# Narrowing the subtracted softmax maximum to one bf16 number, and turning a unit's maxima by one transpose

## What is computed

```python
def _attend(q, k, v):
    sim = jnp.einsum('bhid,bhjd->bhij', q, k) * HD ** (-0.5)
    attn = jax.nn.softmax(sim, axis=-1)
    out = jnp.einsum('bhij,bhjd->bhid', attn, v)
```

## Time and profile before

| what | value |
|---|---|
| runs, median (lowest to highest) | 4588.85 us (4585.59 to 4595.32) |
| span of the profiled execution | 4575.9 us |
| median of the runs less that span | 12.95 us |
| PE busy | 4083.6 us (89%) |
| DVE busy | 3089.2 us (68%) |
| ACT busy | 2075.6 us (45%) |
| POOL busy | 1348.3 us (29%) |
| chain that ended last, by engine | PE 62%, DVE 16%, ACT 6%, issue 5% |

### The profile page before, as it was taken

One profiled execution on the slowest core, in us unless ns is written; L12 is line 12 of the kernel. 1 busy time (PEld: TensorE's weight loads), 2 busy tenths in 40 slices (PEclk: granted clock), 3 DMA queues, 4 the chain that ended last, 5 costly groups with the idle time before them and its releaser, 6 DMA issues.

```text
span 4575.9 us, 56543 instructions
## 1 busy us (share of the span) xinstructions
PE 4083.6 (89%) x20828; PEld 2493.2 (54%) x20828; DVE 3089.2 (68%) x4613; ACT 2075.6 (45%) x3756; POOL 1348.3 (29%) x664
## 2 busy tenths in 40 slices
PE   7999989789998887998999977888999999997889
PEld 5343346633334575555555546667555555546668
DVE  5888856688886666778777854345677777774355
ACT  2555544355565443444444435553344344444541
POOL 1100001100000124655655553421344444451120
PEclk8999989999998998999999988999999999998999
DMA  4223231123222333233223313223322232214220
GB/s 129 40 43 49 44 58 35 43 30 56 40 30 53 63 58 65 64 65 66 60 63 65 65 47 77 70 58 73 69 65 65 61 70 66 58 34 121 67 53 19
DMA packets 154420, 269.87 MB, mean 59 GB/s; under 512 B 36459, under 2 KB 70053, under 8 KB 153121
## 3 DMA queue, kind: packets, MB, share of 16 engines
q1 hardware_dynamic: 154144, 266.25, 27.7%
HBM read 105.01 MB, written 29.64 MB: 29 GB/s over the span
## 4 chain that ended last, share of the span: by engine, by line
PE 62%; DVE 16%; ACT 6%; issue 5%; POOL 4%; SPq 4%; DMA 3%; DVEq 0%; POOLq 0%; ACTq 0%
PE PS L1012 26%; PE PS L1191 12%; PE PS L1088 4%; PE PS L1084 4%; PE PS L1233 3%; PE PS L1321 3%; DVE t L1751 3%; PE PS L1243 2%; SPq L2181 2%; DVE t L1747 2%; POOL t L2042 1%; SPq L2198 1%; ACT t L1487 1%; DMA t<-t 1%; PE PS L1218 1%
## 5 line engine op out<-in xcount | busy, mean ns | idle before, releaser
L1012 PE MATMUL PS<-t 128*128 128x512 f32 (+4 forms) x7896 | 1981.4, 383 | 166.5 <-ACT t L1466 24.9
L1466 ACT ACTIVATE t<-PS 128x512 f32<-128x512 f32 (+2 forms) x1600 | 1166.6, 750 | 1175.6 <-PE PS L1012 1169.8
L1012 PEld LDWEIGHTS PS<-t 128*128 128x128 f32 (+2 forms) x7896 | 1246.0, 187 | 719.5 <-issue 260.2
L1191 PE MATMUL PS<-t 128*32 128x512 f32 (+2 forms) x4352 | 809.1, 610 | 0.2
L1747 DVE TENSOR_REDUCE t<-PS 128x1 fp32r<-128x1024 f32 x512 | 621.7, 1219 | 267.6 <-PE PS L1084 260.9
L1751 DVE TENSOR_REDUCE t<-PS 128x1 f32<-128x512 f32 x1024 | 650.8, 682 | 72.1 <-PE PS L1088 70.8
L2042 POOL TENSOR_TENSOR t<-t 128x1024 f32<-128x1024 f32 x256 | 617.6, 2412 | 130.4 <-ACT t L1466 103.4
L1088 PE MATMUL PS<-t 96*128 96x512 bf16 x1024 | 371.6, 395 | 33.9 <-DVE t L1751 14.8
L1084 PE MATMUL PS<-t 128*128 128x512 f32 x1024 | 338.6, 413 | 56.1 <-DVE t L1747 36.9
L2038 POOL TENSOR_TENSOR t<-t 128x1024 f32<-128x1024 f32 x64 | 155.1, 2424 | 747.5 <-PE PS L1201 448.7
L1191 PEld LDWEIGHTS PS<-t 128*32 128x32 f32 (+2 forms) x4352 | 170.6, 121 | 329.2 <-issue 324.5
(11 more groups left out here) (133 smaller groups left out, 3932.6 us busy)
## 6 DMA issues: line engine op xcount, KB each, us to landing
t<-t SPq DMA_DIRECT2D x640, 128.0 KB, 2.5
t<-scr_n SPq DMA_DIRECT2D x288, 128.0 KB, 6.5
t<-t SPq DMA_DIRECT2D x128, 256.0 KB, 3.9
scr_n<-t SPq DMA_DIRECT2D x72, 256.0 KB, 2.3
t<-t SPq DMA_DIRECT2D x256, 64.0 KB, 2.1
t<-in_L_Wg SPq DMA_DIRECT2D x16, 768.0 KB, 4.6
t<-in_L_W SPq DMA_DIRECT2D x36, 256.0 KB, 3.3
t<-in_L_Wo SPq DMA_DIRECT2D x64, 128.0 KB, 2.6
```

Of the source, the lines that this page charges most:

```text
L1012: ins = e.matmul(out, l, r, start=i == 0, stop=i == len(terms) - 1, tile_position=tp)
L1191: ins = e.matmul(banks[S.ot][wd * j:wd * j + wd, :], u.v[j][kt], P[0:S.pr, j, :], start=kt == 0, stop=kt == S.nkt - 1, tile_position=(0, w ...
L1466: e.activation(dst, src, ACT.Exp, scale=S.L.scale).then_inc(*expd.inc((S.i, i)))
```

## The change

The self and cross stages of layers 0 and 1 keep one bf16 number for the maximum instead of three. The self stages write it directly from the joining `tensor_reduce` (step `mjoin`); the cross stages write it directly from the block reductions, so no step is left between the last of them and the transpose. `MT` has two buffers there instead of one. Contractions go from 99 rows to 97. In all three kinds of stage the maxima of a unit lie side by side as columns of `MT` (16, 32 or 8 of them), one transpose turns them all, and one copy of 128 columns brings them to `MR`. Each partition of `MR` then holds 128 query rows of one head. The DMA of a head gathers four such partitions into one row. In the narrow cross stage one DMA gathers all 32 into the four rows, which lie behind each other on one partition. In the wide stages the maximum stays float32.

```diff
-            S.NM, S.NR = sbt(c, [128, 32]), sbt(c, [128, 32])
-            S.MT = sbt(c, [128, 8, 4, 3], BF16)
-            S.MR = [sbt(c, [12, N], BF16) for _ in range(2)]
+            S.MT = [sbt(c, [128, 32], BF16) for _ in range(2)]
+            S.MR = [sbt(c, [32, 128], BF16) for _ in range(2)]
+            sbt(c, [128, 976])
...
-            S.MT = [sbt(c, [128, S.nqt, 2], F32R) for _ in range(2)]
-            S.MR = [sbt(c, [2, 128 * S.nqt], F32R) for _ in range(2)]
+            S.MT = [sbt(c, [128, 2 * S.nqt], F32R) for _ in range(2)]
+            S.MR = [sbt(c, [2 * S.nqt, 128], F32R) for _ in range(2)]
+            sbt(c, [128, 768])
...
-                u.mrow = [buf[96:99, 0, j, q0:q0 + nw] for j in range(4)] if u.su is u else None
+                u.mrow = [buf[96:97, 0, j, q0:q0 + nw] for j in range(4)] if u.su is u else None
+                if cross and u.mrow:
+                    u.mrow = [buf[96:97, 0, :, :].rearrange("p j n -> p (j n)")]
...
-        return out + [("mparts", S, m), ("mturn", S, m)]
+        return out + [("mturn", S, m)] if S.cross else out + [("mjoin", S, m), ("mturn", S, m)]
...
# TensorE, mturn
+                elif S.cross:
+                    for j, q0 in ((2, 4), (3, 0), (3, 4)):
+                        k, nth = where["max", S.i, m, j, q0]
+                        w.wait_ge(bank_free[k], nth)
                 else:
-                    w.wait_ge(max_part, (S.i, m, "end"))
+                    w.wait_ge(max_part, (S.i, m))
                 w.wait_ge(set_up, "ident")
-                rows, idt = (12, identb) if S.L.style == 16 else (2, ident)
-                for q0 in range(0, S.nqt, 4):
-                    o, k, nth = take(w, small, ("turn", S.i, m, q0))
-                    o = o.bitcast(BF16) if S.L.style == 16 else o
-                    for q in range(4):
-                        if S.L.style == 16:
-                            src = S.MT[:, q0 + q, :, :].rearrange("p j c -> p (j c)")
-                        else:
-                            src = f(S.MT[m % 2][:, q0 + q, :])
-                        ins = e.transpose(o[0:rows, 128 * q:128 * q + 128], src, idt[:, :])
-                    ins.then_inc(*bank_full[k].inc(nth))
+                n = S.nqt * S.nh
+                o, k, nth = take(w, small, ("turn", S.i, m))
+                if S.L.style == 16:
+                    ins = e.transpose(o.bitcast(BF16)[0:n, 0:128], S.MT[m % 2][:, 0:n], identb[:, :])
+                else:
+                    ins = e.transpose(o[0:n, 0:128], f(S.MT[m % 2][:, :]), ident[:, :])
+                ins.then_inc(*bank_full[k].inc(nth))
...
# VectorE, narrow
-                    e.memset(S.QK[0][96:99, 1, :, :], 1.0).then_inc(*zeroed.inc((S.i, 0)))
+                    e.memset(S.QK[0][96:97, 1, :, :], 1.0).then_inc(*zeroed.inc((S.i, 0)))
...
-                e.tensor_reduce(S.NM[:, 8 * j + q0:8 * j + q0 + 4], v, AX.X, ALU.max, negate=True
-                                ).then_inc(*bank_free[k].nth(nth))
-            elif what == "mparts":
+                ins = e.tensor_reduce(S.MT[m % 2][:, 8 * j + q0:8 * j + q0 + 4], v, AX.X, ALU.max, negate=True)
+                ins.then_inc(*bank_free[k].nth(nth))
+            elif what == "mjoin":
...
-                e.tensor_copy(part[0], nm).then_inc(*max_part.inc((S.i, m, 1)))
-                w.wait_ge(max_part, (S.i, m, 1))
-                e.tensor_tensor(nr, nm, part[0], ALU.subtract).then_inc(*max_part.inc((S.i, m, 2)))
-                w.wait_ge(max_part, (S.i, m, 2))
-                e.tensor_copy(part[1], nr).then_inc(*max_part.inc((S.i, m, 3)))
-                w.wait_ge(max_part, (S.i, m, 3))
-                e.tensor_tensor(part[2], nr, part[1], ALU.subtract).then_inc(*max_part.inc((S.i, m, "end")))
+                e.tensor_reduce(S.MT[m % 2][:, 0:n], S.NMX[:, 0:n, :], AX.X, ALU.max, negate=True
+                                ).then_inc(*max_part.inc((S.i, m)))
...
# VectorE, mturn
-                for q0 in range(0, S.nqt, 4):
-                    o, k, nth = full(w, ("turn", S.i, m, q0))
-                    o = o.bitcast(BF16) if S.L.style == 16 else o
-                    e.tensor_copy(mr[:, 128 * q0:128 * q0 + 512], o[0:rows, 0:512]).then_inc(*bank_free[k].nth(nth))
+                o, k, nth = full(w, ("turn", S.i, m))
+                o = o.bitcast(BF16) if S.L.style == 16 else o
+                e.tensor_copy(mr[0:n, :], o[0:n, 0:128]).then_inc(*bank_free[k].nth(nth))
...
# SyncE, mturn
-                per = 3 if S.L.style == 16 else 1
-                mr = S.MR[m % len(S.MR)]
-                for j in range(S.nh):
-                    src, dst = mr[per * j:per * j + per, 0:128 * S.nqt], u.mrow[j]
+                mr = S.MR[m % 2]
+                per = S.nqt if S.L.style == 64 or not S.cross else 4 * S.nqt
+                for i, row in enumerate(u.mrow):
+                    src, dst = mr[per * i:per * i + per, :], row
                     if S.L.style == 64:
                         src, dst = f(src), f(dst)
-                    e.dma_start(dst, src).then_inc(*mrow_in[m % 2].inc((S.i, m), 16))
+                    e.dma_start(dst.rearrange("p (q n) -> p q n", n=128), src).then_inc(*mrow_in[m % 2].inc((S.i, m), 16))
```

More of the change, by code:

```diff
@@ L331, in attention_tiles @@
             T = S.after
-            S.P, S.OR, S.R, S.RE, S.NMX, S.NM, S.NR, S.MT, S.MR, S.NR2 = (
-                T.P, T.OR, T.R, T.RE, T.NMX, T.NM, T.NR, T.MT, T.MR, T.NR2)
+            S.P, S.OR, S.R, S.RE, S.NMX, S.MT, S.MR, S.NR2 = (
+                T.P, T.OR, T.R, T.RE, T.NMX, T.MT, T.MR, T.NR2)
             S.NAT, S.nqk, S.nbuf = T.NAT, 1, 4
@@ L1573, in scalar_program, with turn_read @@
                     w.wait_ge(r, a[0])
+    def turn_read(w, S, m):
+        old, last = (S, m - 2) if m >= 2 else (S.after, len(S.after.sus) + m - 2) if S.after else (None, 0)
+        if old:
+            k, nth = where["turn", old.i, last]
+            w.wait_ge(bank_full[k], nth)
     def vector_program(e, w):
@@ L1743, in vector_program @@
                     if m >= 2:
-                        k, nth = where["turn", S.i, m - 2, 0]
+                        k, nth = where["turn", S.i, m - 2]
                         w.wait_ge(bank_full[k], nth)
                     o, k, nth = full(w, ("max", S.i, m, j, qt))
-                    e.tensor_reduce(S.MT[m % 2][:, qt, j:j + 1], o, AX.X, ALU.max, negate=True
+                    e.tensor_reduce(S.MT[m % 2][:, S.nqt * j + qt:S.nqt * j + qt + 1], o, AX.X, ALU.max, negate=True
                                     ).then_inc(*bank_free[k].nth(nth))
@@ L1759, in vector_program @@
+                ins.then_inc(*bank_free[k].nth(nth))
+            elif what == "mjoin":
                 S, m = a
-                for key in [x for x in where if x[0] == "max" and x[1:3] == (S.i, m)][-3:]:
-                    k, nth = where[key]
+                turn_read(w, S, m)
+                n = S.nqt * S.nh
+                for j, qt, half in ((3, 2, 1), (3, 3, 0), (3, 3, 1)):
+                    k, nth = where["max", S.i, m, j, qt, half]
                     w.wait_ge(bank_free[k], nth)
-                nq = S.nqt
@@ L1764, in vector_program @@
-                n = nq * S.nh
-                if not S.cross:
-                    e.tensor_reduce(S.NM[:, 0:n], S.NMX[:, 0:n, :], AX.X, ALU.max, negate=True
-                                    ).then_inc(*max_part.inc((S.i, m, 0)))
-                    w.wait_ge(max_part, (S.i, m, 0))
-                nm = S.NM[:, 0:n].rearrange("p (j q) -> p j q", q=nq)
-                if m or S.after:
-                    old = S if m else S.after
-                    for q0 in range(0, old.nqt, 4):
-                        k, nth = where["turn", old.i, m - 1 if m else len(old.sus) - 1, q0]
-                        w.wait_ge(bank_full[k], nth)
@@ L1775, in vector_program @@
-                part = [S.MT[:, 0:nq, :, i].rearrange("p q j -> p j q") for i in range(3)]
-                nr = S.NR[:, 0:n].rearrange("p (j q) -> p j q", q=nq)
-                e.tensor_copy(part[0], nm).then_inc(*max_part.inc((S.i, m, 1)))
-                w.wait_ge(max_part, (S.i, m, 1))
-                e.tensor_tensor(nr, nm, part[0], ALU.subtract).then_inc(*max_part.inc((S.i, m, 2)))
-                w.wait_ge(max_part, (S.i, m, 2))
-                e.tensor_copy(part[1], nr).then_inc(*max_part.inc((S.i, m, 3)))
@@ L1782, in vector_program @@
-                w.wait_ge(max_part, (S.i, m, 3))
-                e.tensor_tensor(part[2], nr, part[1], ALU.subtract).then_inc(*max_part.inc((S.i, m, "end")))
+                e.tensor_reduce(S.MT[m % 2][:, 0:n], S.NMX[:, 0:n, :], AX.X, ALU.max, negate=True
+                                ).then_inc(*max_part.inc((S.i, m)))
             elif what == "mturn":
                 S, m = a
-                rows = 12 if S.L.style == 16 else 2
-                mr = S.MR[m % len(S.MR)]
-                if m >= len(S.MR):
-                    w.wait_ge(mrow_in[(m - len(S.MR)) % 2], (S.i, m - len(S.MR)))
```

(16 more changed lines are left out.)

9 lines of the change are left out of this document (5 added, 4 removed).

## The result

The changed kernel takes 4521.9 us (median of four runs, 4514.55 to 4537.6); the kernel before, run beside it, 4587.64 (four runs). The ratio is 0.9854, with a 95% interval of 0.9831 to 0.9877: 65.7 us less. The forecast was 4522, and it was "faster".

The account below looks back on a forecast made before the run. PE was taken to set the pace in narrow self stages, with DVE close behind. Terms 29.4 + 7.7 + 18.7 + 3 + 7.9 = 66.7 us gave a span near 4509 and a run near 4522 us; range 4500 to 4562.

Parts of the forecast that it names:

- The chain of four: Narrow self turns: without the four small DVE instructions after the join, PE's 0.97 us idle goes in most turns; 29.4 us.
- Fewer transposes, narrow self: Narrow self turns: one bf16 transpose stays of four, saving 0.24 us, 32 times; 7.7 us, counted in full.
- Fewer transposes, wide: Wide turns: three of four float32 transposes go, 0.27 us, 64 times; 17.3 us, of which three quarters were counted.
- The Trainium skill's 275 ns a transpose: Alternative price for the 400 transposes that go: worth 110 us, kernel nearer 4430; the prediction said the trace disagrees.
- The copy: DVE's shorter copy of the turned maxima, mostly covered by PE's work in wide stages; 3 us, up to 24 without cover.
- Narrow cross: Narrow cross stages: maxima land earlier, PE's short waits go, long ones shrink, layer norm statistics gain; 7.9 us, between 2 and 25.
- The cover of the DMAs: Narrow self: maxima land at 240.7, the unit's first score is at 245.88, leaving 5.2 us before PE would wait.
- The distance from span to run: Whole kernel: median run lies 12.95 us above the profiled span of 4575.9 us, and this distance was kept.
- Late arrival: Slower rival: 256 B pieces land so slowly that PE waits at narrow units' first scores; 4666 at 10 us landing; chance 4%.
- Taken over: Rival: PE's holes close but the next reduction, ACT or a stack DMA becomes late; 33 us lost, 4556; chance 17%.
- No change: Rival: turns have slack to their unit's start, and a later wait gives all back; 4589; chance 4%.
- More than the sum: Rival: DVE's relief counts in wide and cross stages too, and the clock stays up; about 100 us, 4489; chance 13%.

Follow-up runs that it names:

- one_number: Kernel before with the narrow maximum as one bf16 number, the rest of the turn as before; 4544.7 us, 0.9919 of the kernel before.
- wide_turn: Kernel before with only the wide self stages turning their eight columns of maxima by one transpose and copying 128 columns; 4569.92 us, 0.9974.
- after_again: The changed kernel run once more, unedited, beside ten other runs of the kernel before; 4522.26 us, 0.9868.
- before_again: The kernel before, unchanged, run once more for a second profile; 4595.42 us in one run, span 4593.6 us.

## Why the prediction was right, point by point

- **What bounds the kernel**: right for the narrow self stages. The chain between the join and the transpose was PE's own idle time, and PE got all of it back.
- **The chain of four, 29.4 us**: right. PE's wait for it fell by 30.9 us over the span (38.7 to 7.8), of which 1.3 are the two waits in the cross stages, and `one_number` has 0.97 a turn.
- **Fewer transposes, narrow self, 7.7**: the last one costs 0.15 us, not the 0.08 of its share in a run of four. Measured 0.32 less 0.15, 32 times: 5.4. The same in the cross stages: 0.39 instead of 0.48, so 6.2 of the 7.7 counted ahead of the discount.
- **Fewer transposes, wide, 17.3 less a quarter, 13**: too little by the distances. The last transpose advances PE by 0.03 us, not 0.09, so 0.33 goes, 64 times: 21. And the discount by a quarter, taken from PE's share of the chain, isn't seen in the distances: in layer 3 the full 0.33 reached the stage's end. But the runs of `wide_turn` gained 11 us, 17 at most, so whether the kernel as a whole got the 21 stays open, and the 13 of the forecast fits these runs better.
- **The Trainium skill's 275 ns a transpose** (TensorE: Matmul & The Clock Gate, Part 4, PE-mode transpose) would have asked for 110 us. As a price of removing one in a sequence it fell: the rows show 0.08 to 0.09 each. (With 110 in the place of 7.7 and 18.7 the forecast's own sum gives 4438, not the 4430 that it names.)
- **The copy, 3 us**: its length was right (272 and 209 ns for 290 and 200), its worth was not: no turn distance moved by more than 0.02 us when the copy left DVE.
- **Narrow cross, 7.9 and three quarters of 7.7**, 13.7 together: measured 9.1 and 9.6 us in two profiles, up to the last turn of the stages. That is about what the fewer transposes (6.2), the six short waits (1.4) and the two waits for L1783 (1.3) make. The 3.2 for the layer norm isn't seen: PE's wait for its last DVE step (L1639, 29.8 us in 12 places) is 31.4 and 28.3 us in the changed kernel's two profiles. I took 1 us off each long wait because the maxima would be issued sooner. They stand behind the stack's loads whenever they are issued; the waits are 7.5 and 4.5 us in the changed kernel's profile, 5.9 and 3.8 in `after_again`, 5.9 and 5.4 before.
- **The cover of the DMAs, 5.2 us**: somewhat too small. The 1.81 us run from the start of the last issue, and I added them to its end, so the cover was about 0.6 us more.
- **The sum**: by the distances 29.4 + 5.4 + 9.3 + 21 = 65 in place of 66.7. Too much for copy, cross and narrow transposes, too little for wide ones, and these cancelled. The runs gave 65.7 and 58.8 us in two groups; that they can't confirm the 21 is said above.
- **The distance from span to run**: wrong. I kept 12.95 us between them as if it lay around the span. Every profiled execution whose run time is on record has it 1.8 us above its span (4537.6 and 4535.8, say). For the first profile of before the run time isn't on record; by the same 1.8 it took 4577.7 us, and then the other 11 lie in this execution, which was below the others. So the span came out at 4535.8 and 4524.7, not 4509, while the run time came out right, because the same 12.95 had been on both sides. That it fell within 0.1 us is luck: the interval of the ratio alone is plus or minus 10 us.
- **The rivals.** Late arrival fell: DMAs of 256 B pieces are as quick as a longer row, and the cover held. "Taken over", with 33 us lost, fell: the changed kernel gained 65.7 us, give or take 10, and in the narrow self stages the full chain. For the wide stages a part of it isn't excluded, since 21 us in the distances stand against 6 to 17 in the runs of `wide_turn`. No change fell. More than the sum was not seen: from the first to the last turn of the cross stage of layer 0 the clock was 0.88 in one profile of the changed kernel and 0.85 in the other, against 0.88 before.

Open is how much of the stages' differences comes from the clock and how much from work; the two profiles of each kernel only hint at it. Open too is where the wide turn's missing 4 us or more go in the runs, and why the clock of a cross stage differs from profile to profile. Whether a landing slower than the cover can be had without moving the turn wasn't tried.

## What to carry to other kernels

Look for chains of tiny dependent instructions on one engine for which another stands idle with all else issued: their full length comes back, while shortening work that no engine waits for (the copy) moved nothing that could be measured. Price an instruction that goes by the distance of starts in its own place, and price the one that stays too. A small DMA that a later matmul needs should be issued ahead of bulk loads on its queue; the wait it causes looks like latency, and moving six loads behind it cured it. And take the change's worth from many runs or from medians of distances between landmarks, since two profiles of one program can differ by 18 us in 4580.

## What the runs showed of the hardware

- The next matmul starts 0.15 us after a single transpose of 16 columns of bf16, 0.16 and 0.17 us after one of 32 and 48, but 0.03 us after one of 8 columns of float32 in the wide turn. Why they differ was not tried.
- A DVE instruction of 128 x 16 that writes bf16 takes 174 to 177 ns with its outputs in runs of four or more, and 202 to 230 with each output by itself. A subtraction that only reads such numbers took 174 instead of 186.
- A DMA of bf16 maxima in four pieces of 256 B landed 1.58 to 1.63 us after the start of the last issue, one row of 2 KB 1.65, three rows of 2 KB 1.81. Issued right behind the twelve loads of a query stack, such DMAs took 6.6 to 11.6 us.
- The same program's granted clock was 0.950 in one execution and 0.953 in another, with 17.7 us between the spans. In the cross stage of layer 0, between its first and last turn, it was 0.88, 0.88 and 0.81 in three kernels whose work there is the same (`before`, `before_again`, `wide_turn`).
